# Last edge pass of a graph layer: two walk registers per load instead of six on VectorE and ScalarE, and one small table at another address

## The chip, the cores and the metric

The kernel runs on one core of a Trainium2 chip. The metric is the device time of one launch in microseconds (us). Every time below comes from one profiled execution or from the runs listed beside it.

## The reference, cut to what matters

A graph layer of 6250 nodes with 256 features and 100000 edges, sorted by destination: attention over the edges (8 heads of 32), a linear-attention mixer over the nodes, and a soft mixture of 8 experts.

```python
alpha = jnp.einsum('ehc,ehc->eh', q[dst], k[src] + e) / jnp.sqrt(jnp.float32(OUT_CH))
p = jnp.exp(alpha - m[dst])                       # m: maximum over a node's edges
s = jax.ops.segment_sum(p, dst, num_segments=n)
w = p / (s[dst] + 1e-16)
out = jax.ops.segment_sum((v[src] + e) * w[:, :, None], dst, num_segments=n)
...
x = x + out + skip + mixer(xn)
x = x + experts(_layernorm(x))
```

The change concerns the sum of `(v + e) * p` over each node's edges, and the helper table of the step that carries maxima from one chunk of edges to the next.

## The kernel before, in words

The kernel works in stages: node projections; a first edge pass that gathers keys and values and writes scores; a stage that takes maxima by scans over 16 chunks of edges and turns the exponentials back to edge order; the last edge pass, which sums the values per node; and the experts.

The last edge pass walks over STEPS = 450 steps, a pair of edge tiles (2 x 125 edges) and one node tile in each. It is 75 iterations of `d_body`, each with SU = 6 steps `s` written out; the first iteration is peeled, the others run in hardware loops. Each engine runs its own `d_body`, in its own order, and semaphores join them:

- SyncE (L566 to L569) loads the values of step k from `ve_d` into slot `vg[:, s]`, once VectorE is done with step k-6 (`pv_ready`).
- ScalarE (L1220 to L1232) copies the two edge tiles' weights `p` and destinations into slot `pv[:, s]` (L1226, semaphore `meta_ready`), once TensorE is done with step k-6 (`sum_done`). For steps 1, 3 and 5 it also makes the one-hot matrices (L1216, L1218), two steps later.
- GpSimd (L703, L710) subtracts the node tile's first row from the destinations for steps 1 to 5, and compares for steps 2 and 4. Between iterations 20 and 27 it also rounds one expert weight per iteration (L718).
- VectorE (L1697 to L1711) makes the one-hot matrices of step 0 (L1703), multiplies values by weights (L1706, `pv_ready`), and adds the finished sum of step k-2 from PSUM into the node tile's accumulator (L1695, in the helper `add`).
- TensorE (L968) multiplies one-hot by values, two matmuls a step; it waits for the one-hot, for `pv_ready`, and for the accumulator bank's last reader.

Which edge tiles and which node tile belong to a step depends on the data: it stands in a table of numbers `walk` in partition 0, three rows of WALK = 461 int32, which begins at element 9850 of `region_s` (8200 + 750 + 450 + 450). The tensors allocated ahead of `region_s` have 13200, 12288 and 12680 words a partition. Engines read the table into registers and address with these. In the last pass VectorE loads six registers from row 1, beginning at number `it * 6 + 3`, in step 0 (L1708, L1709), after it has issued the multiply and ahead of `add`; ScalarE loads six from row 2, at `it * 6 + 2`, at the head of an iteration (L1221). The first pass has six-number loads too: L520 (row 0, number 6n), L521 (row 0, 6n + 3), L909 (row 1, 6n), L1176 (row 0, 6n), L1602 (row 2, 6n).
`pick` (L167) holds three small 0/1 tables used in the chunk step (`of_chunk` by VectorE, `of_head` and `to_rows` by TensorE, one small matmul each). It is filled by one DMA after the node stage.

Of the kernel before, what the change touches and what calls it, by code (L numbers as in the profile page):

```python
# [30 lines left out]
H, C = 8, 32  # L31
T = 125
NT, ET = N // T, E_ // T
# [10 lines left out]
SU = 6  # L44
# [3 lines left out]
CH = 16  # L48
# [7 lines left out]
RW = H + 2  # L56
PV = D + H
LAGQ = 5
# [3 lines left out]
LAGP = 2  # L62
LAGV = 6
LAG = 2
# [13 lines left out]
R_GNN, R_MKV, R_BO, R_B2, R_G1, R_E1, R_G2, R_E2, R_BR = 0, 1024, 1536, 1792, 2048, 2304, 2560, 2816, 3072  # L78
# [5 lines left out]
def wait(eng, sem, value):  # L84

    if isinstance(value, int) and value <= 0:
        return
    eng.wait_ge(sem, value)
# [18 lines left out]
def build(nc, a, out):  # L107
    ctx = ExitStack()
    with ctx:
# [21 lines left out]
        with early:  # L131
            weights = early.enter_context(nc.sbuf_tensor("weights", [128, 12288], F32))
            region_r = early.enter_context(nc.sbuf_tensor("region_r", [128, ET * (RW + 2) + ROWS], F32))
# [30 lines left out]
        bo_e = sb("bo_e", [KB, D + 2])  # L164
        ends = sb("ends", [128, 8])
        fence = weights[0:H, 12014:12014 + 10 * CH].rearrange("p (k c) -> p k c", k=10)
        pick = weights[:, 11400:11400 + H + CH + 128]  # L167
        of_head, of_chunk, to_rows = pick[:, 0:H], pick[:, H:H + CH], pick[0:H, H + CH:H + CH + 128]
        ends_c = weights[:, 11600:11600 + 4 * CH].rearrange("p (k c) -> p k c", k=4)
        back_c = weights[:, 11700:11700 + 2 * CH].rearrange("p (k c) -> p k c", k=2)  # L170
# [33 lines left out]
        def carve(start, *shape, parts=128):  # L204

            size = int(np.prod(shape))
            if start is not None:
                used[0] = start
            at = used[0]
            used[0] += size  # L210
            assert used[0] <= 11240, used
            flat = region_s[0:parts, at:at + size]
            if len(shape) == 1:
                return flat
            names = "abcd"[:len(shape)]
            return flat.rearrange(f"p ({' '.join(names)}) -> p {' '.join(names)}",
                                  **{n: s for n, s in zip(names[:-1], shape[:-1])})
# [46 lines left out]
        walk = carve(None, 3, WALK, parts=1).bitcast(I32)  # L264
# [105 lines left out]
        def tile_pair(ref, place):  # L370

            return ref[:, bass.ds(place, 2, CH), :]
# [719 lines left out]
        def _(act):  # L1092
# [37 lines left out]
            regs = [act.alloc_register(f"act_pair{s}") for s in range(SU)]  # L1130
# [81 lines left out]
            def act_hot(it, s):  # L1212

                act.wait_ge(place_ready, it * len(BY_ACT) + BY_ACT[s])
                for w in range(2):
                    i = fn(hot[:, s, w, :], iota[:, :], ACT.Abs, bias=place_in[:, s, w:w + 1], scale=-1.0)  # L1216
                order(i)
                fn(hot[:, s], hot[:, s], ACT.Relu, bias=1.0, scale=-1.0).then_inc(hot_act, 1)  # L1218

            def d_body(it):  # L1220
                act.load(regs, walk[0:1, 2, bass.ds(it * SU + LAGP, SU)])  # L1221
                for s in range(SU):
                    k, behind = it * SU + s, (s - LAGH) % SU
                    place = act.snap(regs[s], min_val=0, max_val=ET - CH - 1)
                    wait(act, sum_done, k - R + 1)
                    copy(pv[:, s, :, D:D + H + 1], tile_pair(rec, place)[:, :, 0:H + 1]).then_inc(meta_ready, 1)  # L1226
                    if behind in BY_ACT and s >= LAGH:
                        act_hot(it, behind)
                    elif behind in BY_ACT and not (isinstance(it, int) and it == 0):
                        act_hot(it - 1, behind)  # L1230
                order.reset()

            def upper_weights(n):
                e, i = n // 3, n % 3
                copy(wxh(i, e).rearrange("p c n -> p (c n)"), wx[i][:, e].rearrange("p c n -> p (c n)")).then_inc(f_wh, 1)

            d_body(0)
            with act.Fori(1, SPLIT - 1) as it:
                d_body(it)
# [5 lines left out]
            for n in range(EARLY):  # L1245
                d_body(SPLIT - 1 + n)
                upper_weights(n)
# [61 lines left out]
        def _(dve):  # L1309
# [197 lines left out]
            regs = [dve.alloc_register(f"dve_walk{s}") for s in range(SU)]  # L1507
# [182 lines left out]
            def add(k, s, reg):  # L1690
                j = dve.snap(reg, min_val=0, max_val=NT - 1)
                dve.wait_ge(sum_done, k + 1)
                wait(dve, acc_done, k)
                to = acc[:, bass.ds(j, 1), :].rearrange("p o f -> p (o f)")
                tt(to, to, psum[0:T, 4 + (s - LAG) % 3, 0:PV], ALU.add).then_inc(acc_done, 1)  # L1695

            def d_body(it):  # L1697
                for s in range(SU):
                    k = it * SU + s
                    dve.wait_ge(meta_ready, k + 1)  # L1700
                    if s in BY_DVE:
                        wait(dve, sum_done, k - SU + 1)
                        stt(hot[:, s], iota[:, :].unsqueeze(1).broadcast_to((T, 2, T)), jb_all[:, bass.ds(k, 1)],  # L1703
                            pv[:, s, :, D + H:D + H + 1].broadcast_to((T, 2, T)), ALU.add, ALU.is_equal).then_inc(hot_dve, 1)
                    dve.wait_ge(v_in[s], it * 16 + 16)
                    tt(pv[:, s, :, 0:D].rearrange("p w (h c) -> p w h c", h=H), vg[0:T, s].rearrange("p w (h c) -> p w h c", h=H),  # L1706
                       pv[:, s, :, D:PV].unsqueeze(3).broadcast_to((T, 2, H, C)), ALU.mult).then_inc(pv_ready, 1)
                    if s == 0:  # L1708
                        dve.load(regs, walk[0:1, 1, bass.ds(it * SU + LAGQ - LAG, SU)])  # L1709
                    if s >= LAG or not (isinstance(it, int) and it == 0):  # L1710
                        add(k - LAG, s, regs[s])  # L1711

            d_body(0)
            dve.wait_ge(acc_zero, 1)
            with dve.Fori(1, SI) as it:
                d_body(it)
# [198 lines left out]
```

## Time and profile before

| what | value |
|---|---|
| median of 3 runs (lowest to highest) | 3412.22 us (3410.17 to 3415.22) |
| the profiled execution | 3411.48 us |
| its span | 3409.4 us |
| VectorE busy over the span | 2794.6 us (82%) |
| TensorE busy over the span | 3125.4 us (92%) |
| last edge pass | about 1964 to 2487 us from the span's start |

PE is TensorE, DVE VectorE, ACT ScalarE, POOL GpSimd, SP SyncE. A busy share is an average over stages; for this change only the last edge pass counts. Where the profile says "idle before <- issue", the engine waited for nothing but its own queue. A chain of waits is followed back from the last instruction; a "q" behind an engine's name is its queue's work. Start times of groups are rounded to 0.1 us where a source line is listed, to 0.01 us in a timeline.

### The profile page before, as it was taken

How to read it: one execution, taken by the hardware profiler on the slowest of the kernel's cores; microseconds unless marked ns; L12 is line 12 of the kernel's file. 1: busy time of each engine (PE TensorE's matmuls, PEld its weight loads, DVE VectorE, ACT ScalarE, POOL GpSimd, SP SyncE). 2: the span in 40 equal slices, each digit the busy share in tenths (PEclk: the TensorE clock that was granted, in tenths of full speed). 3: DMA queues.
4: the chain of work that ended last, by engine and by line, in shares of the span. 5: the costliest groups of instructions: out<-in, count | busy, mean ns of one | idle time of the engine just before them, and what ended most of it. 6: DMA issues, size and time to landing. Idle time of an engine off the chain costs nothing.

```text
span 3409.4 us, 71878 instructions
## 1 busy us (share of the span) xinstructions
PE 3125.4 (92%) x17162; PEld 2443.6 (72%) x17162; DVE 2794.6 (82%) x5782; ACT 1692.1 (50%) x4461; POOL 1670.1 (49%) x1834
## 2 busy tenths in 40 slices
PE   4997999999999999999999488888889999999999
PEld 3776566666666666666666355555579999999999
DVE  6776789888889898888888989989977677776775
ACT  1222334334444343443443356655567777777776
POOL 2222777777777777777777278877710000000000
PEclk9998899999999999999999699999989999999999
DMA  7344999999999999999999377777710000000000
GB/s 185 116 123 140 248 265 268 260 261 265 265 267 267 265 268 263 265 266 264 260 266 261 102 231 224 227 228 226 229 37 15 12 18 12 12 18 12 17 14 9
DMA packets 521332, 592.15 MB, mean 174 GB/s; under 512 B 188089, under 2 KB 397272, under 8 KB 520996
## 3 DMA queue, kind: packets, MB, share of 16 engines
q1 hardware_dynamic: 310638, 347.54, 34.9%
q0 software_dynamic: 202016, 232.77, 26.0%
q10 hardware_dynamic: 8473, 9.56, 0.9%
q8 instruction: 74, 1.21, 0.2%
q14 instruction: 131, 1.07, 0.1%
HBM read 425.33 MB, written 163.37 MB: 173 GB/s over the span
## 4 chain that ended last, share of the span: by engine, by line
PE 49%; DMA 17%; DVE 15%; issue 7%; SPq 5%; POOL 3%; DVEq 3%; ACT 1%; ACTq 0%; POOLq 0%
PE psum L750 10%; PE psum L752 10%; PE psum L751 10%; PE psum L968 8%; DMA weights<-kv_tab,idx 6%; DMA ve_d<-weights 5%; DVE weights L1515 3%; PE psum L812 3%; PE psum L828 2%; DMA region_r<-kv_tab,idx 2%; POOL weights L660 2%; DVE part L1529 2%; DVEq L1709 2%; DVE region_s L1706 1%; DVE kv_more L1515 1%
## 5 line engine op out<-in xcount | busy, mean ns | idle before, releaser
L660 POOL DMA_INDIRECT weights<-kv_tab,idx x450 | 551.9, 1226 | 244.8 <-issue 157.4
L828 PE MATMUL psum<-region_x,weights 125*125 x1800 | 487.2, 394 | 70.1 <-DVE weights L1523 23.4
L968 PE MATMUL psum<-region_s 125*125 125x264 f32 x1800 | 453.5, 401 | 71.6 <-DVE region_s L1706 69.3
L1272 ACT ACTIVATE region_s<-psum,bns 128x250 f32<-128x250 f32 x800 | 402.7, 554 | 229.9 <-PE psum L752 229.9
L812 PE MATMUL psum<-we,weights 64*125 64x256 f32 x1800 | 512.9, 406 | 0.0
L1759 DVE TENSOR_TENSOR parts_h<-region_s,parts_h 128x500 fp32r<-128x500 f32 x400 | 270.6, 682 | 241.4 <-ACT parts_h L1276 207.8
L968 PEld LDWEIGHTS psum<-region_s 125*125 125x125 f32 x1800 | 305.3, 188 | 219.7 <-DVE region_x L1695 64.5
L1142 ACT ACTIVATE weights<-psum,region_s 125x250 f32<-125x250 f32 x450 | 211.1, 469 | 504.3 <-PE psum L820 503.5
L828 PEld LDWEIGHTS psum<-region_x,weights 125*125 125x125 f32 x1800 | 321.9, 190 | 174.2 <-issue 135.2
L812 PEld LDWEIGHTS psum<-we,weights 64*125 64x125 f32 x1800 | 299.0, 185 | 180.7 <-issue 151.8
L660 POOL DMA_INDIRECT kv_more<-kv_tab,idx x300 | 370.5, 1235 | 93.5 <-issue 77.2
L1515 DVE TENSOR_TENSOR weights<-weights,psum 125x1024 f32<-125x1024 f32 x225 | 274.0, 1218 | 57.7 <-DMA weights<-kv_tab,idx 49.2
L1706 DVE TENSOR_TENSOR region_s<-region_s 125x512 f32<-125x512 f32 x450 | 313.6, 697 | 0.5 <-issue 0.5
L710 POOL TENSOR_SCALAR region_s<-iota,region_s 125x125 f32<-125x125 f32 x300 | 280.3, 944 | 14.7
L1276 ACT CAST parts_h<-region_s 128x500 fp32r<-128x500 f32 x400 | 244.1, 610 | 15.1
L750 PE MATMUL psum<-parts_x,wx_up 128*128 128x250 f32 x800 | 231.7, 290 | 2.8 <-DVE wx_low L1751 2.8
L1136 ACT COPY idx<-region_r 125x2 int32 x450 | 85.9, 191 | 295.7 <-DVE part L1529 220.1
L1695 DVE TENSOR_TENSOR region_x<-region_x,psum 125x264 f32 x450 | 189.7, 422 | 48.4 <-issue 43.2
L750 PE MATMUL psum<-wx_up,parts_h 128*125 128x256 f32 x800 | 226.8, 283 | 1.8 <-DVE region_s L1794 1.8
L752 PE MATMUL psum<-wx_up,parts_h 128*125 128x256 f32 x800 | 225.6, 282 | 0.0
L751 PE MATMUL psum<-wx_low,parts_h 128*125 128x256 f32 x800 | 225.4, 282 | 0.0
L752 PE MATMUL psum<-parts_x,wx_low 128*128 128x250 f32 x800 | 225.0, 281 | 0.0
(260 smaller groups left out, 7586.2 us busy)
## 6 DMA issues: line engine op xcount, KB each, us to landing
region_s<-ve_d SPq DMA_DIRECT2D x450, 256.0 KB, 3.0
ve_d<-weights SPq DMA_DIRECT2D x225, 256.0 KB
ve_d<-kv_more SPq DMA_DIRECT2D x150, 256.0 KB
weights<-in_attr_t SPq DMA_DIRECT2D x450, 62.5 KB
ve_d<-region_r SPq DMA_DIRECT2D x75, 256.0 KB
kv_tab<-region_s SPq DMA_DIRECT2D x50, 224.0 KB
region_s<-ab_d SPq DMA_DIRECT2D x450, 1.0 KB
weights<-kv_tab,idx POOLq DMA_INDIRECT x450
```

Source lines behind the costliest of these rows:

```text
L660: nc.gpsimd.indirect_dma_start(kg[r][0:T, w, :], None, kv_tab, bass.IndirectOffsetOnAxis(idx[:, r, w:w + 1], 0)).then_inc(gathered[r], 16)
L710: compared = nc.gpsimd.tensor_scalar(hot[:, s, w, :], iota[:, :], place_in[:, s, w:w + 1], None, ALU.is_equal)
L750: mm(to, lhs[0], rhs[0], start=start, stop=False)
L751: mm(to, lhs[0], rhs[1], start=False, stop=False)
L752: return mm(to, lhs[1], rhs[0], start=False, stop=stop)
L812: last = mm(psum[0:T, s % 2, w * D:(w + 1) * D], att_b[:, s % RP, w * T:(w + 1) * T], we[:, :], start=True, stop=True)
L828: last = mm(psum[0:T, 2 + s % 2, w * D:(w + 1) * D], hott[:, s % RA, w * T:(w + 1) * T], q_all[:, bass.ds(j, 1), :].rearrange("p o d -> p ...
L968: last = mm(bank, hot[:, s, w, :], pv[:, s, w, 0:PV], start=(w == 0), stop=(w == 1))
L1272: last = fn(fh[:, layer, o, :], psum[:, bk + e % 2, o * BN:(o + 1) * BN], ACT.Relu, bias=bns[:, layer, 1, col:col + 1], scale=bns[:, layer ...
L1515: tt(rows4, rows4, psum[0:T, s % 2, :].rearrange("p (w d) -> p w d", w=2).unsqueeze(2).broadcast_to((T, 2, 2, D)), ALU.add).then_inc(kv_ad ...
L1706: tt(pv[:, s, :, 0:D].rearrange("p w (h c) -> p w h c", h=H), vg[0:T, s].rearrange("p w (h c) -> p w h c", h=H), pv[:, s, :, D:PV].unsquee ...
L1759: tt(low[:, e % 2].rearrange("p c n -> p (c n)"), fh[:, layer].rearrange("p c n -> p (c n)"), up[:, e % 2].rearrange("p c n -> p (c n)").b ...
```

## The change

In the last edge pass VectorE and ScalarE load two registers at steps 0, 2 and 4 of an iteration, from the same place in the table as before, instead of six once. `pick` moves from columns 11400 to 11551 of `weights`, which the first pass also uses for its one-hot tiles, to columns in `region_r` that held the mixer's output bias, last read in the node stage. Sizes and number of its readers stay.

```diff
-        pick = weights[:, 11400:11400 + H + CH + 128]
+        pick = region_r[:, ET * (RW + 2) + R_BO:ET * (RW + 2) + R_BO + H + CH + 128]
...
             def d_body(it):
-                act.load(regs, walk[0:1, 2, bass.ds(it * SU + LAGP, SU)])
                 for s in range(SU):
+                    if s % 2 == 0:
+                        act.load(regs[s:s + 2], walk[0:1, 2, bass.ds(it * SU + s + LAGP, 2)])
                     k, behind = it * SU + s, (s - LAGH) % SU
...
-                    if s == 0:
-                        dve.load(regs, walk[0:1, 1, bass.ds(it * SU + LAGQ - LAG, SU)])
+                    if s % 2 == 0:
+                        dve.load(regs[s:s + 2], walk[0:1, 1, bass.ds(it * SU + s + LAGQ - LAG, 2)])
                     if s >= LAG or not (isinstance(it, int) and it == 0):
                         add(k - LAG, s, regs[s])
```

## Rows read from the trace of the kernel before

**Rows 1.** Who waited for whom, 2170 to 2478 us: total us, times, longest.
```profile
ACT region_s L1226 <- PE psum L968: 77.6, 110, 1.6
POOL region_s L703 <- ACT region_s L1226: 71.1, 90, 0.9
DVE region_x L1695 <- issue: 29.1, 43, 1.0
DVE region_x L1695 <- PE psum L968: 1.0, 1, 1.0
PE psum L968 <- ACT region_s L1218: 0.4, 1, 0.4
```

**Rows 2.** VectorE's timeline, iterations at 2312.77 and 2319.96: start, us, instruction, idle.
```profile
2312.77 0.48 DVE L1703 SCALAR_TENSOR_TENSOR region_s<-iota,region_s 125x250 f32<-125x250 f32 x1
2313.16 0.68 DVE L1706 TENSOR_TENSOR region_s<-region_s 125x512 f32<-125x512 f32 x1
2314.83 0.43 DVE L1695 TENSOR_TENSOR region_x<-region_x,psum 125x264 f32 x1 [0.98 <-issue]
...
2315.78 0.42 DVE L1695 TENSOR_TENSOR region_x<-region_x,psum 125x264 f32 x1
2316.12 0.68 DVE L1706 TENSOR_TENSOR region_s<-region_s 125x512 f32<-125x512 f32 x1
2316.72 0.42 DVE L1695 TENSOR_TENSOR region_x<-region_x,psum 125x264 f32 x1
...
2319.96 0.48 DVE L1703 SCALAR_TENSOR_TENSOR region_s<-iota,region_s 125x250 f32<-125x250 f32 x1
2320.35 0.69 DVE L1706 TENSOR_TENSOR region_s<-region_s 125x512 f32<-125x512 f32 x1
2321.43 0.43 DVE L1695 TENSOR_TENSOR region_x<-region_x,psum 125x264 f32 x1 [0.39 <-issue]
...
2326.56 0.48 DVE L1703 SCALAR_TENSOR_TENSOR region_s<-iota,region_s 125x250 f32<-125x250 f32 x1
```

**Rows 3.** Loads by source line (ns min/median/max, starts): whole pass, then two alone.
```profile
L1709 DVEq TENSOR_LOAD <-region_s x75: 809/1401/1436, 1963.9 to 2478.7; - x75
L1709 DVEq TENSOR_LOAD <-region_s x1: 1405/1405/1405, 2313.1 to 2313.1; - x1
L1709 DVEq TENSOR_LOAD <-region_s x1: 816/816/816, 2320.3 to 2320.3; - x1
L1221 ACTq TENSOR_LOAD <-region_s x75: 745/1316/1529, 1962.0 to 2474.6; - x75
```

**Rows 4.** Chain of waits at one aligned load of L1709: start, us, what.
```profile
2306.49 0.75 DVEq L1709
...
2307.64 0.07 DVE region_x L1695
```

**Rows 5.** Loads at other places of the table, by source line.
```profile
L1709 DVEq TENSOR_LOAD <-region_s x1: 1411/1411/1411, 1963.9 to 1963.9; - x1
L1602 DVEq TENSOR_LOAD <-region_s x1: 814/814/814, 388.4 to 388.4; - x1
L1602 DVEq TENSOR_LOAD <-region_s x1: 1596/1596/1596, 408.2 to 408.2; - x1
L1717 DVEq TENSOR_LOAD <-region_s x1: 818/818/818, 2485.0 to 2485.0; - x1
L521 SPq TENSOR_LOAD <-region_s x75: 1267/1307/2496, 334.3 to 1842.0; - x75
L909 PEldq TENSOR_LOAD <-region_s x75: 1466/2193/5820, 334.9 to 1836.9; - x75
```

**Rows 6.** Queue instructions of the helper's register step, 2300 to 2307 us.
```profile
L1691 DVEq MOVE  x5: 36/36/36, 2301.2 to 2304.7; - x5
```

**Rows 7.** Busy time, two stretches: PE, PEld, DVE, ACT, POOL, granted clock, DMA share, GB/s.
```profile
2104.00:2168.00 64.00, 54.58 (x215) 35.88 (x213) 61.64 (x117) 40.67 (x142) 61.17 (x92) 1.00 0.73 219
2175.00:2478.00 303.00, 263.61 (x1056) 177.56 (x1056) 272.94 (x572) 179.32 (x663) 224.43 (x397) 1.00 0.76 228
```

## The prediction

> **What bounds the kernel now.** I read the list of waits of the last edge pass first, because a busy share over the whole span mixes stages. In 308 us of it VectorE waited 29.1 us for its own queue in 43 places and 1.0 us for TensorE; TensorE waited 0.4 us for ScalarE's one-hots, and ScalarE and GpSimd spend 77.6 and 71.1 us waiting on work that follows VectorE's pace [rows 1]. So VectorE with its queue sets the pace, and the others have slack. Next VectorE's timeline [rows 2]: a step without a load goes multiply (L1706), add (L1695) in a fixed cadence: add starts at 2315.78 and 2316.72, 0.94 us a step, of which 0.60 us lies from the multiply's start to the add's and 0.34 us from the add's to the next multiply's. Step 0 is different: with the load in it the add starts 1.67 us behind the multiply in one iteration (2313.16 to 2314.83) and 1.08 us in the next (2320.35 to 2321.43). That is 1.07 and 0.48 us more than 0.60. The two iterations last 7.19 and 6.60 us (starts 2312.77, 2319.96, 2326.56), 6.90 on average.
>
> Third, the loads themselves [rows 3]: these two took 1.405 and 0.816 us. A load begins at about the start of the multiply and runs beside it; behind its end stand register steps and waits until the add, 0.33 us: in the chain of waits one load begins at 2306.49 and its add at 2307.64, 1.15 us later, of which the load takes 0.82 [rows 4]; the add being 1.08 us behind its multiply, the load begins 0.07 us ahead of that. So a load of duration d in step 0 costs d - 0.34 us: 1.07 and 0.48, mean 0.77 us an iteration. That is what there is to win or to lose.
>
> **Why the load has two durations.** The alternation is strict over the pass, and it follows the address. L1709 begins at word 9850 + 461 + 3 + 6 it = 10314 + 6 it of the region, which itself begins at a multiple of four words: even iterations begin 2 words behind a multiple of four, odd ones on it. The first load (it = 0) took 1.411 us [rows 5], and long and short alternate from there. That it isn't the parity of the iteration is shown by L1602, word 10772 + 6n: there the third load (n = 2, on a multiple of four) took 0.814 us and the fourth 1.596 us; and by L1717, word 10764, a multiple of four, 0.818 us. Loads that begin at odd words (L521, L909) are never at 0.8 us: their minima are 1.267 and 1.466 us. The simplest reading: on a multiple of four words the first four come in one read and the other two singly, elsewhere all six come singly. With a fixed part b and a read of r, b + 3r = 0.82 and b + 6r = 1.40, so r = 0.19 and b = 0.24 us (an estimate from these rows).
>
> **The change part by part.** No row shows a load of two words, so its duration d2 is bounded: from above by the six-word load at its two addresses, 0.82 us (aligned) and 1.40 us (not); from below by 0.34 us, under which step 0 costs nothing. By the reading above, two single reads give d2 = 0.24 + 0.38 = 0.62 us, at either address; I take this, since it rests on both rows; a proportional share of the long load, 2/6 of 1.40, is 0.47 us.
>
> The Trainium skill ("Runtime: NRT & Kernel Launch", section Instruction fetch mechanics) says a TENSOR_LOAD costs about 200 ns per register even in bulk. The six-register loads here took 0.82 or 1.40 us, not one value near 1.2 us, so the rule alone does not hold, though its figure is near r. It would make a two-register load 0.40 us, and by the terms below the time 3363 us.
>
> VectorE, step 0: one load of six becomes one of two: 0.77 us falls to 0.62 - 0.34 = 0.28 us.
>
> VectorE, steps 2 and 4: two loads are added. Their place is kinder than step 0's, because no one-hot instruction comes ahead and the queue runs ahead of the engine: the register step L1691, where the load would go in, now stands some 0.45 us before the next multiply's start (the five run from 2301.2 to 2304.7, one each 0.94 us, and the multiply behind the adds starts 0.34 us behind each add) [rows 2, 6]. After the address step of some 0.1 us (a queue instruction of 0.06 and its gap) the load starts 0.25 to 0.35 us ahead of the multiply; with 0.33 us behind it and the add due at 0.60, it is free up to d = 0.52 to 0.62 us. At 0.62 it costs 0 to 0.10 us, say 0.05 each, 0.10 in sum. Behind the waiting queue stand only the add and the next multiply; after a load the queue regains its lead within one step, as it does now behind step 0 [rows 2].
>
> Sum for VectorE: 0.28 + 0.10 = 0.38 us against 0.77: 0.39 us less an iteration, a period of 6.51 us.
>
> Is something else late next? GpSimd is 74% busy in the ordinary iterations (224.43 of 303 us), ScalarE 59%, TensorE 87% with its ends modelled; the 16 DMA engines 76% at 228 GB/s [rows 7]. 6% more pace leaves all of these below full. Only in the nine iterations from 2104 to 2168 us, where GpSimd rounds weights too, is it 61.17 of 64 us busy: there it is the bound at 7.11 us a period, and I count 0.1 us of gain each.
>
> ScalarE: one load of 0.75 or 1.33 us (1.04 on average) at the iteration's head becomes three of some 0.56 us each, 0.6 us more queue time in an iteration of which it waits over 2 us: ScalarE waited 77.6 us for TensorE in some 45 iterations, and more on GpSimd [rows 1]. Queued behind each load are the copies of two steps, which TensorE's release lets run several steps ahead of VectorE's need. I cost it at nothing; without that cover it would cost 0.6 us an iteration, 40 us. The very first load, 1.529 us [rows 3], is in the chain before the pass has begun; two words less four reads save about 0.8 us there, once.
>
> The table `pick`: same DMA, same three small readers, values don't change durations: nothing.
>
> Total: 66 iterations x 0.39 = 25.7, 9 x 0.1 = 0.9, the start 0.8: 27 us less. Against the profiled execution's own 3411.48 us that is 3384 us; the median of the runs is 0.7 us higher than it.
>
> **The rivals.** (B) Reads are cheaper than I take them, d2 up to 0.52 us: the two-word load is one read of 8 bytes, or goes in proportion (0.47 us). Then steps 2 and 4 are free and step 0 costs 0.13 us at 0.47: 0.64 us won, 66 x 0.64 + 1.7 = 44 us, 3367 us. At d2 = 0.34 it is 0.77 x 66 + 1.7 = 52 us, 3359 us. For it: loads begin at even words, so 8 bytes never straddle. The Trainium skill's figure above points here too. Against: the long load at an even word shows no such wide reads.
>
> (C) Most of a load is fixed, one round trip of about 0.8 us whatever the count. Then step 0 costs 0.48 and steps 2 and 4 cost 0.20 to 0.30 each, 0.98 in sum against 0.77: 0.21 us lost, 66 x 0.21 = 14 us, 3425 us: slower. It decides from d2 = 0.75 us, where (d2 - 0.34) + 2 (d2 - 0.57) = 0.77. For it: 0.82 us for four words more is not much; against: 0.58 us lie between two loads of the same size, so the reads do count.
>
> (D) The extra 0.58 us off a multiple of four is a fixed penalty, on top of (C). The new loads begin at words 2, 0, 2 and 0, 2, 0 modulo 4 in turn, so half of them pay it: even iterations 1.06 + 0.25 + 0.83, odd 0.48 + 0.83 + 0.25, mean 1.85 us against 0.77; 75 x 1.08 = 81 us, 3492 us.
>
> (E) VectorE's queue gets faster, but another resource holds the period near 6.9: GpSimd, whose waits are 71.1 us now, or the values' DMA. Then 3405 to 3412 us. Against: the sum of waits, and that five of six steps already run at 0.94 us with no wait for a transfer.
>
> **How the numbers follow.** My case (d2 from 0.53 to 0.72 us, 3372 to 3405 us) 0.46; B 0.22; C 0.15; E 0.12; D 0.05. A measurement here tells about 0.2%, 7 us, from no change. Faster: my case, B and a quarter of E, 0.71; same: the rest of E, 0.09; slower: C and D, 0.20. The range reaches from B's lower part, 3361, to just over C, 3428, and leaves D and the edges of B and C out.
>
> **What would show it.** In the profile after: 225 loads at L1709's successor, near 0.62 us at both addresses (alternation gone or small); the step-0 add 0.88 us behind its multiply, in steps 2 and 4 0.60 to 0.70 us; an iteration of 6.5 us; GpSimd's nine iterations near 7 us as before; ScalarE's waits on TensorE shorter by some 0.6 us an iteration, none of TensorE on ScalarE. A load over 0.75 us would make the forecast wrong in sign; one under 0.5 us, in size. Waits of VectorE or TensorE on GpSimd, ScalarE or a transfer would speak for E.

## The result and the profile after

The changed kernel is slower: 3442.86 us (median of 10 runs, 3428.70 to 3459.52) against 3414.22 us (10 runs), a ratio of 1.0082 (1.0065 to 1.0098), 28 us more. I had forecast 3384 us and a gain.

The profiled execution took 3449.20 us with a span of 3447.1 us. The difference lies in the last edge pass, and it is no matter of the clock: TensorE's granted clock was 1.00 from 1973 to 2478 us in both. The pass's length can be read from the source rows of VectorE's one-hot, which runs once in each of the 75 iterations; here and below the columns of such rows are ns min/median/max, then first and last start. Before, then after:

```profile
L1703 DVE SCALAR_TENSOR_TENSOR region_s<-iota,region_s x75: 475/479/929, 1963.9 to 2478.4; 125x250 f32<-125x250 f32 x75
```
```profile
L1704 DVE SCALAR_TENSOR_TENSOR region_s<-iota,region_s x75: 466/479/926, 1963.5 to 2512.9; 125x250 f32<-125x250 f32 x75
```

From first to last, 514.5 us became 549.4, 34.9 of the 37.7 us by which the spans differ. The source rows of the loads in the kernel after (lines have moved by one or two):

```profile
L1710 DVEq TENSOR_LOAD <-region_s x224: 523/529/551, 1964.3 to 2516.9; - x112
L1223 ACTq TENSOR_LOAD <-region_s x225: 481/495/694, 1962.4 to 2514.8; - x113
```

A load of two words takes 0.53 us on VectorE and 0.49 us on ScalarE at either address, less than the 0.62 and 0.56 us that I had worked with. VectorE's timeline shows what my sum for it promised (an iteration begins at 2300.72):

```profile
2300.72 0.48 DVE L1704 SCALAR_TENSOR_TENSOR region_s<-iota,region_s 125x250 f32<-125x250 f32 x1 [0.30 <-issue]
2301.12 0.68 DVE L1707 TENSOR_TENSOR region_s<-region_s 125x512 f32<-125x512 f32 x1
2301.91 0.43 DVE L1696 TENSOR_TENSOR region_x<-region_x,psum 125x264 f32 x1
...
2303.20 0.68 DVE L1707 TENSOR_TENSOR region_s<-region_s 125x512 f32<-125x512 f32 x1
2303.80 0.42 DVE L1696 TENSOR_TENSOR region_x<-region_x,psum 125x264 f32 x1
...
2306.21 0.68 DVE L1707 TENSOR_TENSOR region_s<-region_s 125x512 f32<-125x512 f32 x1
2307.56 0.43 DVE L1696 TENSOR_TENSOR region_x<-region_x,psum 125x264 f32 x1 [0.66 <-PE psum L968]
2308.28 0.48 DVE L1704 SCALAR_TENSOR_TENSOR region_s<-iota,region_s 125x250 f32<-125x250 f32 x1 [0.30 <-issue]
```

Step 0's add comes 0.79 us behind its multiply (1.67 or 1.08 us in [rows 2]), step 2's (2303.20 to 2303.80) comes at the bare cadence of 0.60 us with a load in it. But at the end the add stands 1.35 us behind its multiply, VectorE waits for TensorE, and the iteration lasts 7.56 us. Who waited for whom in the settled part of the pass, 2170 to 2500 us (total us, times, longest), to be held against [rows 1]:

```profile
POOL region_s L703 <- ACT region_s L1227: 81.4, 44, 1.9
ACT region_s L1216 <- POOL region_s L703: 73.8, 87, 1.3
DVE region_x L1696 <- PE psum L968: 28.8, 44, 0.7
PE psum L968 <- ACT region_s L1218: 28.7, 77, 0.6
PE psum L968 <- POOL region_s L710: 20.3, 74, 0.4
```

TensorE now waits for one-hots, 49 us where it was 0.4 us, and ScalarE and GpSimd wait for each other. GpSimd's side of that stands in [rows 1] (71.1 us); ScalarE's was smaller in the kernel before, in the same 308 us of [rows 1]:

```profile
ACT region_s L1216 <- POOL region_s L703: 23.0, 45, 0.9
```

The chain of waits of the kernel after shows how (start, us, what; one turn of the loop, from one wait of GpSimd to the next):

```profile
2301.93 0.19 POOL region_s L703
...
2303.32 0.19 POOL region_s L710
...
2304.32 0.70 POOL region_s L703 x2
...
2306.23 0.94 POOL region_s L710
...
2307.33 0.20 POOL region_s L703
2307.55 0.70 ACT region_s L1216 x2
2308.27 0.05 ACT region_s L1218
2308.36 0.49 ACTq L1223
...
2309.05 0.05 ACT region_s L1227
...
2309.51 0.19 POOL region_s L703
```

GpSimd subtracts for step 2 (2301.93), compares for step 2, subtracts for 3 and 4, compares for step 4, and only then subtracts for step 5 (2307.33). That releases ScalarE's one-hot of step 5 (2307.55). Behind it in ScalarE's queue, as the program is written, stand the new load (0.49 us) and the copy of step 2 (2309.05), which GpSimd needs to begin again (2309.51). One turn is 7.58 us, and the iteration is as long (7.56 us). This is the loop theory: two engines release each other in turn, and the iteration can't be shorter than one turn. The rivals were GpSimd's longer compares alone, the number of loads in ScalarE's queue, and the table's new address.

### The profile page after: what moved, and what is told of

Same layout as the page of the kernel before. It is cut to its first block, busy times and chain, and to the rows that moved or that the text cites. A ratio compares the mean times of both kernels' runs of the same rounds, so it can differ in the third digit from the quotient of the medians.

```text
span 3447.1 us, 72457 instructions
## 1 busy us (share of the span) xinstructions
PE 3147.4 (91%) x17162; PEld 2447.6 (71%) x17162; DVE 2805.4 (81%) x5782; ACT 1710.9 (50%) x4461; POOL 1689.7 (49%) x1834
## 4 chain that ended last, share of the span: by engine, by line
PE 40%; DMA 18%; DVE 13%; issue 10%; POOL 8%; SPq 5%; ACT 3%; ACTq 1%; POOLq 1%; DVEq 1%
PE psum L750 10%; PE psum L752 10%; PE psum L751 10%; DMA ve_d<-weights 7%; DMA weights<-kv_tab,idx 6%; POOL region_s L710 3%; DVE weights L1516 3%; POOL region_s L703 2%; PE psum L812 2%; PE psum L828 2%; POOL weights L660 2%; DMA region_r<-kv_tab,idx 2%; DVE part L1530 2%; ACT region_s L1216 2%; DVE kv_more L1516 1%
## 5 line engine op out<-in xcount | busy, mean ns | idle before, releaser
L968 PE MATMUL psum<-region_s 125*125 125x264 f32 x1800 | 472.9, 400 | 87.5 <-ACT region_s L1218 43.4
L710 POOL TENSOR_SCALAR region_s<-iota,region_s 125x125 f32<-125x125 f32 x300 | 307.8, 1035 | 14.7
L883 PE MATMUL psum<-region_s,weights 128*128 128x250 f32 x800 | 224.0, 404 | 1.8 <-ACT region_s L1166 1.8
```

The costliest lines, as they stand in the source:

```text
L710: compared = nc.gpsimd.tensor_scalar(hot[:, s, w, :], iota[:, :], place_in[:, s, w:w + 1], None, ALU.is_equal)
L968: last = mm(bank, hot[:, s, w, :], pv[:, s, w, 0:PV], start=(w == 0), stop=(w == 1))
```

## The experiments

The experiments ran in three groups, each with runs of the kernel before beside them, at 3413.70, 3439.24 and 3414.84 us (the last two on the same chip). So ratios within a group are compared, and the length of the pass, read as above from the first to the last start of VectorE's one-hot.

**One engine's loads at a time, and the table alone.** Edits are against the kernel after, if not said otherwise. ScalarE's new loads with VectorE's old one:

```diff
-                    if s % 2 == 0:
-                        dve.load(regs[s:s + 2], walk[0:1, 1, bass.ds(it * SU + s + LAGQ - LAG, 2)])
+                    if s == 0:
+                        dve.load(regs, walk[0:1, 1, bass.ds(it * SU + LAGQ - LAG, SU)])
```

> ScalarE has the new three loads of two, VectorE keeps its one load of six; the table is at its new place. Loop theory: the pass is held by a loop between GpSimd and ScalarE, in which GpSimd's last subtraction of an iteration releases ScalarE's one-hot of step 5, behind that stand ScalarE's load of step 2 (0.49 us) and its copy of step 2, which GpSimd waits for before it begins its compares. With the load in it the loop is 7.0 to 7.3 us, as compares run at 0.95 to 1.05 us beside the unchanged VectorE: 3420 to 3440 us, with TensorE waiting on one-hots. Compare theory: only VectorE's lost idle time, which lets its multiply lie over more of GpSimd's compares, costs: then this kernel stays at 3412 to 3417 us.

Measured: 3424.18 us against 3413.70, ratio 1.0036 (1.0021 to 1.0051); pass 524.8 us. ScalarE's loads alone make the kernel slower, as the loop theory has it. But the compares took 0.88 us, no longer than before, and the iterations alternate 7.30 and 6.93 us, where before they did 7.19 and 6.60: VectorE's own long load, 1.40 us in every other iteration, still counts.

VectorE's new loads with ScalarE's old one:

```diff
+                act.load(regs, walk[0:1, 2, bass.ds(it * SU + LAGP, SU)])
                 for s in range(SU):
-                    if s % 2 == 0:
-                        act.load(regs[s:s + 2], walk[0:1, 2, bass.ds(it * SU + s + LAGP, 2)])
```

> VectorE has the new three loads of two, ScalarE keeps its one load of six at the head of the iteration; the table is at its new place. Loop theory: without the load of step 2 in it the loop is 7.57 less 0.57, 7.0 us, while VectorE alone could do some 6.2: 3405 to 3422 us, TensorE still waiting on one-hots at times, GpSimd's compares at 1.05 us or more. Compare theory: GpSimd alone sets the pace through longer compares, 3435 to 3455 us as in the kernel after.

Measured: 3404.32 us against 3413.70, ratio 0.9974 (0.9955 to 0.9993); pass 504.4 us. VectorE's half of the change is a gain, cut short by one-hots: TensorE still waited 24.7 us for ScalarE's between 2170 and 2465 us. The halves give +0.36% and -0.26%, together +0.1%, while the whole change gives +0.8%: they work on each other.

The kernel before with the table at its new place:

> Only the small table moves. Both theories, and my prediction: nothing, 3412 to 3417 us. If the table's place is the cause, 3430 us or more.

Measured: 3415.33 us against 3413.70, ratio 1.0004 (0.9989 to 1.0019); pass 513.8 us. The table's place costs nothing.

**The same three loads at other places.** ScalarE loads at the odd steps, for the two steps that follow:

```diff
+                if isinstance(it, int) and it == 0:
+                    act.load(regs[0:2], walk[0:1, 2, LAGP:LAGP + 2])
                 for s in range(SU):
-                    if s % 2 == 0:
-                        act.load(regs[s:s + 2], walk[0:1, 2, bass.ds(it * SU + s + LAGP, 2)])
+                    if s % 2 == 1:
+                        n = (s + 1) % SU
+                        act.load(regs[n:n + 2], walk[0:1, 2, bass.ds(it * SU + s + 1 + LAGP, 2)])
```

> The kernel after, but ScalarE makes its three loads at steps 1, 3 and 5 for the two steps that follow, ahead of the copy and of the wait for GpSimd's subtraction, so that no load stands between the one-hot and the copy of the next even step. Loop theory: the load is hidden in ScalarE's wait, the loop is 7.0 us: 3405 to 3422 us. Rival, that the number of ScalarE's loads and not their place costs: 3435 to 3455 us as in the kernel after.

Measured: 3390.68 us against 3413.70, ratio 0.9936 (0.9914 to 0.9958); pass 493.3 us. As many loads in each iteration, of the same size and near the same duration (0.48 to 0.51 us): only their place changed, and the loss became a gain. The number of loads is refuted as the cause.

Fewer loads, four words at step 0, two at step 4 and none at step 2:

```diff
-                    if s % 2 == 0:
-                        act.load(regs[s:s + 2], walk[0:1, 2, bass.ds(it * SU + s + LAGP, 2)])
+                    if s in (0, 4):
+                        n = 4 if s == 0 else 2
+                        act.load(regs[s:s + n], walk[0:1, 2, bass.ds(it * SU + s + LAGP, n)])
```

> The kernel after, but ScalarE loads four words at step 0 and two at step 4: one load less, and none at step 2, between the one-hot of the step before and the copy that GpSimd waits for. Loop theory: the loop is rid of 0.57 us, ratio to the kernel before 0.993 to 0.999. If what counts is how long ScalarE's loads are in sum (1.1 to 1.4 us here against 1.5), ratio 1.004 to 1.008.

Measured: 3390.24 us against 3414.84, ratio 0.9933 (0.9918 to 0.9949); pass 493.2 us, the same as with the odd loads. With the loads at steps 0 and 4 still in their places, it is the one at step 2 that costs.

**Opening the loop on GpSimd's side.** The subtractions of steps 3 and 5 go ahead of the compares of 2 and 4 (`place(s)` holds the wait and the subtraction of step s, `compare(s)` its two compares):

```diff
...
+                place(1)
+                for s in (2, 4):
+                    place(s)
+                    place(s + 1)
+                    compare(s)
```

> The kernel after, with GpSimd's subtraction of steps 3 and 5 put ahead of the compares of steps 2 and 4, not behind them; same instructions, same number. Loop theory: ScalarE's one-hots of steps 3 and 5 are released some 2.2 us earlier, the loop no longer closes over both pairs of compares, and VectorE sets the pace again at 6.3 to 6.5 us an iteration against 7.42: 3372 to 3392 us. Rival, that ScalarE's queue is simply full with three loads: no change from the kernel after, 3435 to 3455 us.

Measured: 3410.21 us against 3439.24, ratio 0.9921 (0.9903 to 0.9939), by which 3414.22 us would become 3387; pass 483.8 us, iterations of 6.36 us. ScalarE's three loads are where the change put them, and the loss is gone. Now GpSimd itself is late: TensorE waited 19.8 us for its compares between 2190 and 2470 us, and ScalarE's one-hots are not among its waits. The order has a price where GpSimd also rounds weights: seven iterations there last 7.47 to 7.50 us, against 6.93 to 6.98 in the kernel after.

The early subtractions and the odd loads together:

> Both cures together: ScalarE's loads at the odd steps, and GpSimd's early subtractions. Loop theory: VectorE's floor, 6.3 to 6.45 us an iteration, 3370 to 3388 us, little better than either cure alone. If a second loop, through TensorE's release of the slots, holds at 6.6 us as in the kernel with the odd loads alone, 3388 to 3395 us.

Measured: 3404.55 us against 3439.24, ratio 0.9906 (0.9888 to 0.9924); pass 481.3 us, iterations of 6.32 us at first and 6.36 later. Of the kernels that do all of the work it is the fastest, but it is not told apart from the early subtractions alone.

The early subtractions with VectorE's new loads and ScalarE's old one:

> VectorE's three loads, ScalarE's old single load, and GpSimd's early subtractions. With the loop open GpSimd itself is the bound at some 6.5 us, as in the kernel after with the early subtractions: ratio 0.990 to 0.994. If ScalarE's three loads still cost there, 0.985 to 0.989.

Measured: 3382.85 us against 3414.84, ratio 0.9921 (0.9899 to 0.9944); pass 483.2 us. With the loop open, one ScalarE load of six or three of two make no difference.

The early subtractions in the kernel before:

> The kernel before (with the table at its new place) with GpSimd's early subtractions. If VectorE's queue sets the pace there and not the loop, nothing: ratio 0.997 to 1.001, iterations of 7.2 and 6.6 us in turn. If the loop held already in the kernel before, ratio under 0.995.

Measured: 3413.28 us against 3414.84, ratio 0.9999 (0.9987 to 1.0011); pass 516.3 us, iterations of 7.19 and 6.60 us as in [rows 2]. The loop did not hold the kernel before; VectorE's queue did.

**What GpSimd's compares add.** In the kernel after they are longer. The groups of L710 between 2190 and 2400 us (busy us, mean ns), before and after:

```profile
L710 POOL TENSOR_SCALAR region_s<-iota,region_s 125x125 f32<-125x125 f32 x123 | 117.2, 962 | 6.0
```
```profile
L710 POOL TENSOR_SCALAR region_s<-iota,region_s 125x125 f32<-125x125 f32 x111 | 121.3, 1102 | 5.4
```

Four compares an iteration, 0.14 us more each: 0.56 us of the loop. The next kernel leaves out the second compare of steps 2 and 4 from the second iteration on (`range(2 if isinstance(it, int) and it == 0 else 1)` in place of `range(2)`):

> The kernel after with GpSimd's second compare of steps 2 and 4 left out from the second iteration on, so half of those one-hots stay what they were: some 2.1 us less in the loop of 7.57. Loop theory: VectorE alone sets the pace, 6.3 us an iteration: 3362 to 3385 us. If ScalarE or VectorE's added loads hold the period by themselves, no more than 10 us less than the kernel after: 3430 to 3450 us.

Measured: 3405.43 us against 3439.24, ratio 0.9910 (0.9891 to 0.9929); pass 477.9 us, iterations of 6.32 us. That the compares are in the loop is shown. What is left is VectorE's own pace: it has no waits in the list from 2190 to 2455 us.

Another kernel has all its compares, but its multiply treats only four of the eight heads from the second iteration on:

```diff
-                    tt(pv[:, s, :, 0:D].rearrange("p w (h c) -> p w h c", h=H), vg[0:T, s].rearrange("p w (h c) -> p w h c", h=H),
-                       pv[:, s, :, D:PV].unsqueeze(3).broadcast_to((T, 2, H, C)), ALU.mult).then_inc(pv_ready, 1)
+                    some = H if isinstance(it, int) and it == 0 else H // 2
+                    tt(pv[:, s, :, 0:some * C].rearrange("p w (h c) -> p w h c", h=some), vg[0:T, s, :, 0:some * C].rearrange("p w (h c) -> p w h c", h=some),
+                       pv[:, s, :, D:D + some].unsqueeze(3).broadcast_to((T, 2, some, C)), ALU.mult).then_inc(pv_ready, 1)
```

> The kernel after, but VectorE's multiply treats only the first four heads from the second iteration on, half its length; the other heads' sums are then not what they should be. VectorE has slack in the kernel after, so its own pace is not at stake. If GpSimd's compares wait while a multiply reads two operands from SBUF, and so lengthen the loop, the compares fall from 1.04 to 0.75 us or less and the iteration by four times that, to 6.3 to 6.6 us: ratio to the kernel before 0.980 to 0.993. If the multiply does not matter to GpSimd, compares stay at 1.04 us and the ratio at 1.005 to 1.010.

Measured: 3356.74 us against 3414.84, ratio 0.9836 (0.9815 to 0.9857); pass 456.4 us, iterations of 6.07 us. GpSimd's compares, 2190 to 2400 us:

```profile
L710 POOL TENSOR_SCALAR region_s<-iota,region_s 125x125 f32<-125x125 f32 x138 | 104.1, 764 | 6.8
```

With the shorter VectorE instruction GpSimd's compares are shorter by 0.34 us each. Four times that, 1.35 us, would bring the loop of 7.57 us to 6.22, already below the 6.32 at which the full multiply runs; so down to 6.32 the compares alone can account for the gain, and the rest, to 6.07, took a shorter multiply on VectorE itself. The Trainium skill ("SBUF — State Buffer", section Who interferes with whom) says that a VectorE instruction with two SBUF inputs contends with a GpSimd instruction that reads SBUF. The trace agrees: the multiply has both inputs in SBUF, and compares went from 1.10 to 0.76 us as it was halved. How the engines share is not shown here, only that the compares follow the multiply.

**What a load costs.** VectorE loads four words, one and one, ScalarE (not shown) three at steps 0 and 3:

```diff
-                    if s % 2 == 0:
-                        dve.load(regs[s:s + 2], walk[0:1, 1, bass.ds(it * SU + s + LAGQ - LAG, 2)])
+                    if s in (0, 4, 5):
+                        n = 4 if s == 0 else 1
+                        dve.load(regs[s:s + n], walk[0:1, 1, bass.ds(it * SU + s + LAGQ - LAG, n)])
```

> The kernel after with other sizes of load: VectorE four words at step 0, one at step 4, one at step 5; ScalarE three at steps 0 and 3. My reading of the prediction, 0.24 us and 0.19 us for each read with a four-word read on a multiple of four words: one word 0.43 us, three words 0.76 us on ScalarE, four words 0.43 or 1.0 us. The other reading, 0.23 us and 0.29 us a read with two words in one read on an even word, as the two-word loads of 0.53 us suggest: one word 0.53 us, three words 0.8 us, four words 0.53 us on a multiple of four, 0.8 to 1.1 us elsewhere.

Measured, by source rows: the four-word load that begins two words behind a multiple of four, the four-word load that begins on a multiple of four, a one-word load, and ScalarE's loads of three words:

```profile
L1711 DVEq TENSOR_LOAD <-region_s x1: 978/978/978, 1999.6 to 1999.6; - x1
L1711 DVEq TENSOR_LOAD <-region_s x1: 358/358/358, 2006.4 to 2006.4; - x1
L1711 DVEq TENSOR_LOAD <-region_s x1: 308/308/308, 2003.7 to 2003.7; - x1
...
L1223 ACTq TENSOR_LOAD <-region_s x150: 693/703/907, 1983.4 to 2487.0; - x150
```

With 0.53 us for two words and 1.40 for six, singles cost 0.09 us and 0.22 per word: 0.31, 0.53, 0.97 and 1.41 us for one, two, four and six words. A four-word load on a multiple of four costs 0.36 us in all, and six words there 0.36 + 0.44 = 0.80 us, against 0.82 measured. So the first reading's structure was right (four words in one read on a multiple of four, singles elsewhere) and its two constants were off; the second reading is refuted, as one word takes 0.31 us and not 0.53. The about 200 ns per register of the Trainium skill ("Runtime: NRT & Kernel Launch", section Instruction fetch mechanics), which it states of loads that the runtime puts in, is near the 0.22 us per word of the singles here and does not hold for the wide read. This kernel ran once, at 3421.61 us, so I read its loads and not its time; its pass of 501.9 us, with no ScalarE load at step 2, is shorter than before as well.

## Why the prediction was wrong, point by point

- What bounds the kernel before, VectorE with its queue: right. With the loop opened it did not move (0.9999).
- The two durations of the six-word load follow the address: right, and the structure of the reading with it.
- The terms of the sum for VectorE: step 0 costs d - 0.34 = 0.19 us at the measured 0.53 (0.79 - 0.60 in the timeline), forecast 0.28; steps 2 and 4 cost nothing, forecast 0 to 0.10 us. VectorE's period by these is 6.90 - 0.77 + 0.19 = 6.32 us, and where nothing else binds (one compare left out) it ran at 6.32 us. I had 6.51.
- The step that failed is "Is something else late next?", in both its halves. "I cost it at nothing" for ScalarE's loads rested on how long ScalarE waits in sum. But only a wait that ends behind a load covers it. The wait for GpSimd's subtraction of step 5 ends ahead of the load of step 2, and behind that load stands the copy that GpSimd needs; so its 0.49 us lengthen the turn. The price I named for lost cover, 0.6 us an iteration or 40 us, is near the 35 us by which the pass grew, but by luck: it was the sum of ScalarE's added queue time, and the settled iteration, 7.57 us where VectorE alone needs 6.32, was held by a loop that I had not counted, with 0.49 us of one load and 0.56 us of longer compares added to it.
- "6% more pace leaves all of these below full" compared busy shares. In the kernel after GpSimd waits 81.4 us of 330 and still sets the pace with ScalarE: a loop over two engines has a length of its own, which no share shows. The row for it stood in front of me: GpSimd waited 71.1 us for ScalarE's copy L1226 [rows 1], and I read that as slack that follows VectorE's pace, without following what the copy waits behind.
- I took GpSimd's durations as given. They depend on VectorE's multiply: 0.76 us for a compare with half of it, 1.10 with all of it.
- Of the rivals, B had VectorE's side more nearly right than mine; E came nearest in kind (another resource holds the period), but I let it hold the old period and no worse; the actual case, a loop longer than that, was not among them. C and D, the cases for slower, named the wrong cause: loads are short.
- The start of the pass: ScalarE's first load fell from 1.529 to 0.694 us, as forecast.
- GpSimd's nine iterations with the rounding, forecast near 7 us: 6.93 to 6.98 us in six of them, right.
- The table: nothing, right.

What stays open. The loop without its load and with the old compares would be 7.58 - 0.49 - 0.56 = 6.53 us by this estimate, under the 6.90 of before; with only one of the two it would be 7.0 to 7.1 us. So most of the loss needs both at once, which fits the halves' not adding up. But why the compares grow only when both halves are there (0.88 and 0.79 us with one alone, 1.10 with both) was read and not tested; I take it to be how the two engines' rhythms fall against each other. The same may be behind the two regimes in the kernel after, 7.7 and 6.7 us in turn in the first 20 iterations and 7.57 us behind the stretch with GpSimd's rounding, and behind the spread of its ten runs, 31 us where the kernel before has 11 (19 to 26 us in the other groups, which have more runs); that is argued only. The odd loads' kernel runs at 6.46 us in its first third and 6.63 later, above VectorE's 6.32, and what holds it there was not taken apart.

A version that beats both kernels: early subtractions with the odd loads, ratio 0.9906 (0.9888 to 0.9924) to the kernel before, some 32 us less.

## What to carry to other kernels

Before work is added to an engine with slack, ask what each of its waits waits for and who waits for the instruction behind it: work placed behind a wait on another engine lengthens a loop that goes back to that engine, while the same work ahead of the wait was hidden here (the same loads, ratio 1.0082 or 0.9936 by their place). Issue what releases another engine before long work of one's own, as the two early subtractions show (1.6% between the kernel after and the same kernel with them). Compare the length of loops over engines with the bound that is being removed, not busy shares.

## What the runs showed of the hardware

A TENSOR_LOAD from SBUF took 0.31 us for one word and 0.22 us for each further one, but 0.36 us for four words that begin on a multiple of four words: six words cost 0.82 or 1.40 us by their address alone. A GpSimd compare of 125 x 125 took 1.10 us on average in the kernel after and 0.76 us in the kernel that differs from it only in VectorE's multiply, of half the length.
